# A macaron block on one core: where the router's logits stand in the first job of the feed-forward

## The reference, cut to what matters

```python
x = x + 0.5 * ffn(layernorm(x))
x = x + mixer(layernorm(x))      # Mamba-like, 16 heads of 64
x = x + 0.5 * ffn(layernorm(x))

def ffn(x):
    shared = silu(x @ Ws_gate) * (x @ Ws_up) @ Ws_down         # 704 wide
    scores = softmax(x @ W_router)                             # 8 experts: the logits
    vals, idx = top_k(scores, 2)
    h = silu(x @ We_gate[e]) * (x @ We_up[e])                  # per expert, 352 wide
    return sum over the two chosen experts of vals * (h @ We_down[e]) + shared
```

## Time and profile before

| | us |
|---|---|
| median of 3 runs | 1470.63 (1470.34 to 1471.83) |
| profiled execution, its own time | 1477.63 |
| its span | 1475.6 |
| PE busy | 1413.8 (96%) |
| DVE busy | 976.0 (66%) |
| POOL busy | 826.3 (56%) |
| ACT busy | 780.0 (53%) |
| mean granted clock of TensorE | 0.987 |

### The profile page before, as it was taken

One profiled execution on the slowest core, in us unless ns is written; L12 is line 12 of the kernel. 1 busy time (PEld: TensorE's weight loads), 2 busy tenths in 40 slices (PEclk: granted clock), 3 DMA queues, 4 the chain that ended last, 5 costly groups with the idle time before them and its releaser, 6 DMA issues. The chain is left out here.

```text
span 1475.6 us, 23088 instructions
## 1 busy us (share of the span) xinstructions
PE 1413.8 (96%) x8754; PEld 1220.8 (83%) x8754; DVE 976.0 (66%) x1680; ACT 780.0 (53%) x1289; POOL 826.3 (56%) x496
## 2 busy tenths in 40 slices
PE   6999999999999899999999999889999999999998
PEld 5877999998987777788778779669879999998887
DVE  6484445445557898889879879966755444455466
ACT  3313666666632366575756656744115666666511
POOL 3202888887735544834753663662016887877543
PEclk9899999999999999999999999999999999999999
DMA  8232777777754220021012011006135877777444
GB/s 322 86 121 88 254 291 284 266 267 277 260 164 114 86 83 19 16 72 44 1 58 72 2 44 58 10 32 243 38 124 185 300 258 284 296 274 276 143 133 171
DMA packets 66782, 225.74 MB, mean 153 GB/s; under 512 B 7536, under 2 KB 15728, under 8 KB 65264
## 3 DMA queue, kind: packets, MB, share of 16 engines
q1 hardware_dynamic: 44592, 166.58, 31.4%
q0 software_dynamic: 11360, 37.23, 8.2%
q10 hardware_dynamic: 10720, 20.45, 3.7%
HBM read 187.01 MB, written 37.22 MB: 152 GB/s over the span
## 5 line engine op out<-in xcount | busy, mean ns | idle before, releaser
L651 POOL TENSOR_TENSOR g_lo<-g_raw,g_hi 128x1408 fp32r<-128x1408 f32 x54 | 187.8, 3478 | 95.3 <-ACT g_hi L819 92.7
L651 POOL TENSOR_TENSOR u_lo<-u_raw,u_hi 128x1408 fp32r<-128x1408 f32 x54 | 174.5, 3231 | 40.1 <-ACT u_hi L819 40.1
L681 POOL DMA_INDIRECT xg<-token_x,row_of x78 | 110.2, 1413 | 140.4 <-DVE row_of L1299 123.6
L1849 PE MATMUL bank<-u_hi,xgT 128*128 128x352 f32 x624 | 168.4, 333 | 0.0
L1849 PE MATMUL bank<-g_hi,xgT 128*128 128x352 f32 x624 | 162.7, 323 | 0.0
L1872 PE MATMUL bank<-d_hi,hT 128*128 128x512 f32 (+1 forms) x468 | 158.3, 392 | 4.7 <-DVE hT L1154 4.7
L1154 DVE TENSOR_TENSOR hT<-bank,hT 128x384 fp32r<-128x384 f32 x78 | 43.5, 557 | 165.8 <-ACT hT L819 165.8
L1154 DVE TENSOR_TENSOR d_lo<-d_raw,d_hi 128x1536 fp32r<-128x1536 f32 x54 | 130.3, 2413 | 21.1 <-ACT d_hi L819 13.3
L864 ACT ACTIVATE gate<-bank 128x512 f32<-128x512 f32 (+1 forms) x48 | 28.7, 597 | 216.7 <-PE bank L1802 199.1
L737 POOL TENSOR_TENSOR w_hl<-w_raw,w_hl 128x1024 fp32r<-128x1024 f32 x35 | 89.8, 2567 | 90.3 <-ACT w_hl L819 90.3
L1817 PE MATMUL bank<-d_hi,hT 128*128 128x512 f32 x352 | 116.7, 401 | 4.6 <-DVE xs L1154 2.2
(11 more groups left out here) (262 smaller groups left out, 3475.0 us busy)
## 6 DMA issues: line engine op xcount, KB each, us to landing
d_raw<-in_w_down SPq DMA_DIRECT2D x54, 768.0 KB, 5.8
g_raw<-in_w_gate SPq DMA_DIRECT2D x54, 704.0 KB, 6.6
u_raw<-in_w_up SPq DMA_DIRECT2D x54, 704.0 KB, 6.8
w_raw<-in_w_in SPq DMA_DIRECT2D x36, 512.0 KB, 3.7
routed_y<-ys ACTq DMA_DIRECT2D x32, 512.0 KB
token_x<-xn SPq DMA_DIRECT2D x8, 1024.0 KB, 5.7
X<-in_x SPq DMA_DIRECT2D x4, 1024.0 KB, 10.4
turned_x<-tmpT SPq DMA_DIRECT2D x16, 256.0 KB, 4.1
```

The lines of the kernel that those rows point to most:

```text
L651: pool.tensor_tensor(half_of(piece, 1, s), raw_at[piece][s % RING][:], half_of(piece, 0, s).bitcast(F), ALU.subtract)\
L681: pool.indirect_dma_start(xg[:, n % XG], None, token_x, bass.IndirectOffsetOnAxis(ap=row_of[:, at:at + 1], axis=0))\
L1849: ins = pe.matmul(dst[:, 0:FE], xgT[:, n % 2, hx, kc], half_of(piece, hw, NS + j)[:, kc], start=(m == 0), stop=(m == 3 * KD - 1))
```

## The change

The logits of job 0 are placed anew. Each part gets two row tiles: the first is issued in the middle of the part, after 6 of its 12 matmuls (`amid`, a new argument of `gate_up`), the second at its end, ahead of the transposes. Tiles 12 to 15 stay in `last_logits`. Before, the numbers of tiles after the six parts were 4, 0, 2, 2, 2 and 2. The wait for `n_wlo` moves with tile 0 into the middle of part 0. And each f32 matmul of an unsplit tile becomes two, on stationary columns 0 to 63 and 64 to 127, which write rows 0 to 63 and 64 to 127 of `bank[4]`.

```diff
-    LOGITS_AT = [range(0, 4), (), range(4, 6), range(6, 8), range(8, 10), range(10, 12)]
+    LOGITS_AT = [(2 * part, 2 * part + 1) for part in range(6)]
     LOGITS_LAST = range(12, NT)
...
                         if t >= 2 * TB:
-                            ins = pe.matmul(bank[4][:, at:at + NE], tmpT[t - 2 * TB][:, c], wr[:, c],
-                                            start=(c == 0), stop=(c == KD - 1))
+                            for r in range(0, P, P // 2):
+                                ins = pe.matmul(bank[4][r:r + P // 2, at:at + NE], tmpT[t - 2 * TB][:, c, r:r + P // 2],
+                                                wr[:, c], start=(c == 0), stop=(c == KD - 1))
...
                 def router(half):
 
+                    logits(LOGITS_AT[half][1])
+                    transpose_x(PAIRS[half])
+
+                def router_first(half):
+
                     if half == 0:
                         pe.wait_ge(n_wlo, 1)
-                    for t in LOGITS_AT[half]:
-                        logits(t)
-                    transpose_x(PAIRS[half])
+                    logits(LOGITS_AT[half][0])
...
+                            if amid and n == 3 * KD // 2 - 1:
+                                amid(2 * c + part)
...
-                                beside=router if job == 0 else place if job == PLACE_JOB else None)
+                                beside=router if job == 0 else place if job == PLACE_JOB else None,
+                                amid=router_first if job == 0 else None)
```

More of the change, by code:

```diff
@@ L1781, in ranks, with gate_up @@
                     ins.then_inc(n_rank, 1)
-                def gate_up(job, c, par, s0, x_of, width, beside=None):
+                def gate_up(job, c, par, s0, x_of, width, beside=None, amid=None):
                     s = (job - j0) // 2 % NS
```

## The result

| | before | after |
|---|---|---|
| median of 5 runs, us | 1471.64 (1470.34 to 1472.18) | 1464.51 (1461.80 to 1464.89) |
| profiled execution, its own time | 1477.63 | 1462.33 |
| its span | 1475.6 | 1460.3 |
| mean granted clock | 0.987 | 0.994 |

The ratio is 0.9939, 95% interval 0.992 to 0.9959: faster by 9.0 us (6.0 to 11.8). The two medians themselves lie 7.1 us apart. The forecast was 12.7 us and 1457.9, with a range up to 1465.5, so the measured time lies near its upper end. Between the two profiled executions the gap is 15.3 us, more than forecast. That spread is the main thing this case has to teach, and the experiments come back to it.

What follows compares the result with a forecast made beforehand. PE, busy 96% of the span, was taken to set the time in job 0. First pass 8.1 plus second 6.3 make 14.4, less 1.7: 12.7 us, so 1470.63 becomes 1457.9 us, range 1453.5 to 1465.5.

Steps and rivals of the forecast that it cites:

- Column tiles: Eight unsplit tiles of logits in each pass of job 0: 6.9 us become 4.5, saving 2.4 us a pass.
- The cuts in the middle: Six further cuts inside parts of job 0: cost nothing, bounds 0.1 us gain or loss for each.
- First half, second pass: Job 0 up to 1009.06 us: 3.4 us of half clock goes, PE waits some 0.5 us, gain 2.8 us.
- First half, first pass: First dense matmul to part 2: 16.0 us becomes 14.6, gain 1.4, with the clock rising at about 24 us.
- The bound of 3 us for a later rise: First half, first pass: gain of 0 if the clock's rise comes 3 us later still.
- From the last dense matmul to `ranks`: End of job 0: 12.3 us in both passes with a 0.5 us wait, gaining 6.9 and 3.7 us.
- Whether the clock falls at the end: End of job 0: one fall of 3.4 us in one of the two passes, taking 1.7 us back.
- rival B: Clock falls at the end of job 0 in both passes for 6.8 us, rises late at start: about 1464, 17%.
- The step that nothing behind job 0 has a clock of its own: Weight loads, gathers and mixer start by semaphores raised in step, so job 0's gain reaches the end.
- It stands 7.0 us above the median of the runs, and I carry the difference over: Profiled execution, 1477.63 to 1464.9 us, set against the median: 1470.63 - 12.7 = 1457.9 us.
- Rival F: No change: median runs lack the profiled one's half clock stretches, and column tiles bring nothing: 1470, 3%.
- Rival D: Another engine becomes the bound: DVE's rows and POOL's low weights keep their times in the second pass: 1462, 8%.

Runs made afterwards that it cites:

- e3: Kernel before with the column-tiled matmul only, logits placed as before: 1462.86 us, ratio 0.9934.
- e4: Changed kernel with both tiles of each part at its end, none in the middle: 1460.90 us, ratio 0.9911.
- e5: Changed kernel again, unedited, beside more executions of the kernel before: 1463.59 us, ratio 0.9925.
- e9: Changed kernel with its moving side repeated (64 columns in the column tiles, 128 in the first matmul of each split pair): 1462.17 us, ratio 0.9921.
- e2: Changed kernel with the old 128-column matmul, so the spreading of logits alone: 1469.93 us, ratio 0.9972.
- e7: Kernel before, no column tiles, moving side repeated to 128 columns except in the second matmul of each split pair: 1465.17 us, ratio 0.9944.
- e1: Kernel before once more, unedited, with span and granted clock of each execution: 1473.80 us, ratio 0.9997.
- e10: Changed kernel with both tiles of each part at its end and the moving side repeated: 1459.05 us, ratio 0.9903.
- e6: Changed kernel with cuts in the middle of parts 0 and 1 only, both tiles at the end of parts 2 to 5: 1459.38 us, ratio 0.9910.
- e8: Kernel before with column tiles, logits placed as before, moving side repeated to 64 columns (128 for first matmuls of split pairs): 1460.05 us, ratio 0.9913.

## Why the prediction was right in its direction and too large

**Column tiles: right.** 2.4 us a pass forecast from the mixer's rows. Measured at full clock, e3 against before: parts 2 to 5 18.76 to 18.19 and the tail from the last dense matmul to `down` 6.33 to 4.35, 2.55 us. The MM costs 0.029 us. The Trainium skill (TensorE: Matmul & The Clock Gate, LDWEIGHTS) gives a weight load P / 1.2 ns; taken one after the other that doesn't bound pairs of column tiles, of which one starts every 0.058 us here. Its other rule, that a change of tiling mode drains TensorE (TensorEngine Tiling (Array Packing), Key Properties), fits the trace: the first MM of another form starts 0.13 us behind the last column tile, and the way in costs 0.1.

**The cuts in the middle: wrong, costed at nothing.** In parts 2 and 3 that is nearly so: 10.83 us in the change, 10.77 in e4. But a lone column-tiled tile in part 4 takes 0.73 us (part 4 is 5.15 us, less 2.84 dense and 0.85 transposes, for two), not 0.62, so parts 2 to 5 lost 0.63 us a pass where I had 0.16. Against the same tiles in pairs the cuts cost more: 19.39 us for parts 2 to 5 and 4.19 from there to `down`, against 18.19 + 4.35 in e4, 1.0 us a pass.

**First half, second pass: right.** 11.4 us, forecast 11.2. The wait on `xn` was 0.43 us (forecast 0.5).

**First half, first pass: the place right, the size open.** The forecast 14.6 us assumed a rise of the clock near 24 us. Profiles of the change, of e5 and of e9 show 11.2, 16.9 and 14.3, with the first rise at 15.0, 29.2 and 23.6 us; that the middle of the three is near the forecast is chance. The launch starts at half clock (16 transposes from 10.98 on take 3.71 us, 0.23 each, and 0.11 later). That a tile of logits in the middle of part 0 can hold it there is not shown, though it fits: of the six profiles with that cut three had their first rise at 23.6 us or later, and of the eight without it none had it later than 20.7. The bound of 3 us for a later rise was too small.

**From the last dense matmul to `ranks`: right.** 12.16 us in both passes, forecast 12.3. The 0.5 us wait of `ranks` wasn't there: table load 5.84 us behind the last dense matmul and 6.03 from the exponential to `r_sum` are 11.9, just inside PE's own 12.16, which was forecast at 11.8.

**Whether the clock falls at the end: better than costed, and not by the spreading.** I took one fall in two passes; there was none in two profiles of the change. But e2 has the change's placement and falls in both passes, and e3 has the old placement and doesn't. So it is the column tiles, not the spreading, that took the falls at the end away. The prediction had given both reasons against rival B, and only its second, the shorter last piece, can be it. That the shorter run is what matters isn't shown: in e7 the run kept its length, its moving side was wide, and the falls went too.

**The sum.** On the profiled execution the forecast was 12.7 us and 15.3 came, from terms that missed on both sides. The first half of the first pass gave 4.8 us where 1.4 was forecast, as the clock was up early, and that of the second 2.6 for 2.8. Parts 2 to 5 lost 1.3 in both passes for 0.4. What lies behind them gave 10.7 for 10.6, and the fall that was to take 1.7 back didn't come. That is 16.8 us in job 0. The step that nothing behind job 0 has a clock of its own was wrong: 1.9 us of it was lost between the jobs, where the changed kernel's profile has 17.1 us at half clock and that of the kernel before 10.2. These two stretches had the full clock before:

```profile
486.00:489.50 3.50, 3.50 (x14) 2.92 (x12) 2.70 (x5) 1.18 (x3) 0.00 (x0) 0.51 0.00 0
922.90:929.90 7.00, 6.09 (x76) 5.78 (x73) 7.00 (x9) 2.64 (x10) 3.92 (x3) 0.51 0.00 1
```

The last 0.3 us is an earlier start of job 0. On the median, what failed is the last step, "It stands 7.0 us above the median of the runs, and I carry the difference over". The 7.0 us weren't a fixed cost of that execution but half clock, as e1 shows: executions near 1471 us have less of it (0.993 against 0.987). So part of the gain was already in the runs behind that median. Against the wider sample of 1473 to 1475 the change gains 9 to 11 us (e5). The size of 12.7 lies outside the first interval (6.0 to 11.8) and inside the second (7.5 to 14.4). Rival F had this mechanism, with too low a chance and coupled to another. The measured 1464.5 is also the price of rival B, but B's falls came only in e2.

**Where the 9 to 11 us are from.** The full-clock times of job 0 give 2.5 us a pass for the column tiles, less 1.0 a pass for the cuts and about 0.5 for the wait on `xn`: some 2 us in all. The rest, 7 to 9 us, I put down to half clock that went. It is in line with e7's 8, and with the mean clocks, 0.9896 over the 14 executions of before beside e5 and 0.9960 over e5's six: the difference, 0.0064 of 1473 us, makes an estimate of 9.4 us, which is on the high side, as the half clock at the start is in neither.

**Versions whose medians beat both.** e10 at 1459.05 us (ratio 0.9903) and e6 at 1459.38 (0.9910): column tiles, both tiles of parts 2 to 5 at the end of their part, and in the first half a wide moving side or the cuts. The two intervals overlap with each other, with those of e4 and e8 and with that of e5, so which is best stays open. Rival D's mechanism, another engine late in the second pass, begins to show there: e8 has a new wait of PE on DVE's `xn` behind part 4, 0.70 us up to 1010.33, and e10's part 4 takes 5.05 us in the second pass against 4.86 in the first.

## What to carry to other kernels

Read the granted clock beside each row of PE, and look at what went ahead of each fall: here matmuls that load 128 columns of weights to move 8 or 16 cost twice, in their own time and in the clock of what follows. Before spreading such work, shorten it (column tiles, in runs and not one by one, as each run pays some 0.2 us to go in and out) or repeat its moving side while the weight load is the longer of the two. And never carry the distance of one profiled execution from a median over as a constant when its clock differs from theirs.

## What the runs showed of the hardware

- Column tiles of 64 with f32 operands: 0.029 us an MM with 8 and with 64 moving columns alike (e10: 64 MMs from 48.19 on in 2.0 us with the way out), where one 128-column MM takes 0.106 to 0.112.
- Moving 128 columns in place of 8 behind a 128-column f32 weight load costs nothing: 32 MMs in 3.49 us in both kernels.
- The same program on the same inputs takes 1466.7 to 1479.1 us in 48 executions, with mean clocks of 0.994 to 0.986. Which falls come differs by execution; a profile is one draw. In the mixer too: the changed kernel's profile has falls at 486.1 to 489.5 and 922.9 to 929.9 that the kernel before didn't have, and a shorter one near 690 (3.4 us for 6.8).
- Ahead of the first recorded change of the clock the granted clock reads 1.00, though the dense matmuls there take twice their time (e5, 16 to 29 us), so the mean clock of such an execution is too high.

What stays open: why the clock rises at 15 us in one execution and at 29 in another of the same kernel, and how often each comes, since each kernel had one or two profiles.
